# Layer 1's gates by extra product columns instead of elementwise GpSimd products, and its output bias by a one-row matmul

## The reference, cut to what matters

```python
local = _local_attention(heads(q), heads(k), heads(v))      # [B, H, S, 16]
...
lattn = jax.nn.softmax(lscores, axis=-1)
lat_out = jnp.einsum('bhsl,bhld->bhsd', lattn, rv)
remote = lat_out @ rout_w + rout_b
remote_h = remote.reshape(B, S, N_HEADS, HEAD_DIM).transpose(0, 2, 1, 3)
gate = jax.nn.sigmoid(local @ gl_w + remote_h @ gr_w)       # one number per token and head
mixed = gate * local + (1.0 - gate) * remote_h
mixed = mixed.transpose(0, 2, 1, 3).reshape(B, S, D)
return mixed @ out_w + out_b
```

## Time and profile before

| | |
|---|---|
| median of 3 runs | 1696.48 us (1692.83 to 1697.11) |
| the profiled execution | 1699.13 us |
| its span, first to last instruction | 1697.3 us |
| mean granted TensorE clock | 0.890 |
| busy: PE, DVE, ACT, POOL | 1348.5, 968.0, 602.7, 351.2 us |
| layer 1 | from about 924 us to the end |

### The profile page before, as it was taken

How to read it: one execution, slowest core, us unless ns; L and a number is a source line. 1 busy time by engine, 2 the same in 40 slices (tenths; PEclk the granted TensorE clock), 3 DMA queues, 4 the chain that set the end, 5 groups by cost and what they waited for, 6 DMA issues and landing times. The chain is left out here.

```text
span 1697.3 us, 24704 instructions
## 1 busy us (share of the span) xinstructions
PE 1348.5 (79%) x8765; PEld 849.9 (50%) x8765; DVE 968.0 (57%) x2253; ACT 602.7 (36%) x1137; POOL 351.2 (21%) x326
## 2 busy tenths in 40 slices
PE   4479898888888898309995699898989898988753
PEld 1234454454544454208995355646464646454532
DVE  4365555656555653505776166666766675666723
ACT  0034343434343445005552134343434343434331
POOL 2110111110111100161112221233333333312232
PEclk9789999999899989658998689899989998999866
DMA  3441315152522400482221432304040404030000
GB/s 121 115 114 46 94 45 135 45 135 73 121 81 53 100 21 2 157 264 75 75 60 41 131 97 64 95 32 107 33 106 31 108 33 107 24 94 14 2 13 13
DMA packets 70920, 130.40 MB, mean 77 GB/s; under 512 B 7936, under 2 KB 60816, under 8 KB 67344
## 3 DMA queue, kind: packets, MB, share of 16 engines
q1 hardware_dynamic: 67728, 120.42, 25.8%
q0 software_dynamic: 3072, 8.41, 1.8%
HBM read 84.19 MB, written 43.81 MB: 75 GB/s over the span
## 5 line engine op out<-in xcount | busy, mean ns | idle before, releaser
L473 DVE TENSOR_REDUCE first_maxima<-bank 128x1 f32<-128x512 f32 (+3 forms) x352 | 221.3, 638 | 243.4 <-PE bank L306 242.8
L427 ACT ACTIVATE arena<-pair 128x512 f32<-128x512 f32 x320 | 184.2, 598 | 338.2 <-PE pair L335 336.9
L1422 DVE TENSOR_REDUCE second_maxima<-bank 128x2 f32<-128x512 f32 (+1 forms) x224 | 152.7, 685 | 185.5 <-PE bank L1138 182.9
L1293 ACT ACTIVATE second_probs<-pair 128x512 f32<-128x512 f32 (+1 forms) x256 | 137.6, 541 | 307.9 <-PE pair L1162 299.1
L303 PE MATMUL bank<-first_k_stack,first_q_stack 96*128 96x256 bf16 (+3 forms) x512 | 131.8, 311 | 55.7 <-DVE first_maxima L473 36.0
L284 PE MATMUL bank<-first_xT,w_qkv 128*128 128x512 f32 x256 | 131.2, 640 | 17.0 <-DVE first_halves L458 12.9
L328 PE MATMUL pair<-first_q_stack,first_k_stack 99*128 99x512 bf16 (+3 forms) x512 | 125.5, 307 | 8.6 <-DMA first_q_stack<-first_m_turned 8.0
L540 POOL TENSOR_TENSOR first_halves<-first_halves 128x512 f32<-128x512 f32 x32 | 40.5, 1265 | 388.0 <-DVE first_halves L458 388.0
L1159 PE MATMUL pair<-second_q_stack,second_k_stack 99*128 99x256 bf16 (+1 forms) x512 | 99.5, 278 | 2.3 <-ACT second_probs L1293 2.3
L1136 PE MATMUL bank<-second_k_stack,second_q_stack 96*128 96x256 bf16 (+1 forms) x512 | 93.8, 278 | 8.5 <-DMA second_k_stack<-parked 6.6
L1162 PE MATMUL pair<-logits,constants_bf 128*128 128x512 bf16 (+1 forms) x256 | 98.2, 384 | 0.0
(11 more groups left out here) (313 smaller groups left out, 2509.1 us busy)
## 6 DMA issues: line engine op xcount, KB each, us to landing
parked<-first_parts SPq DMA_DIRECT2D x32, 384.0 KB, 2.8
first_q_stack<-parked SPq DMA_DIRECT2D x48, 256.0 KB, 5.0
first_k_stack<-parked SPq DMA_DIRECT2D x48, 256.0 KB, 8.0
parked<-second_parts SPq DMA_DIRECT2D x32, 384.0 KB, 2.5
second_q_stack<-parked SPq DMA_DIRECT2D x48, 256.0 KB, 5.0
second_k_stack<-parked SPq DMA_DIRECT2D x48, 256.0 KB, 7.9
sorted_x<-first_zero SPq DMA_DIRECT2D x3, 1670.5 KB, 11.7
expert_xs<-sorted_x SPq DMA_DIRECT2D x39, 128.5 KB, 2.3
```

Of the source, the lines that this page charges most:

```text
L427: act.activation(PT[:, s:s + len(heads), lo:lo + each], ex[n % 3][:, 0:len(heads) * each].rearrange("p (h q) -> p h q", h=len(heads)), ACT ...
L473: dve.tensor_reduce(nm[:, i, qt, heads[0]:heads[0] + len(heads)], mx[n % 2][:, 0:wide].rearrange("p (h k) -> p h k", h=len(heads)), AX.X, ...
L1293: act.activation(PT[:, s:s + len(heads), lo:lo + each], ex[n % 2][:, 0:len(heads) * each].rearrange("p (h q) -> p h q", h=len(heads)), ACT ...
L1422: dve.tensor_reduce(nm[:, i, qt, heads[0]:heads[0] + len(heads)], mx[n % 2][:, :].rearrange("p (h k) -> p h k", h=len(heads)), AX.X, ALU.m ...
```

## The change

The gate needs `local @ gl` and `remote @ gr`. Both are linear, so they are now made by TensorE as further columns:

- At the start VectorE forms, from the loaded weights, the value weights times gl (`wvg`, 16 columns for each of two chunks), `rout` times gr (`rout_g`), and both biases' products (`b_vg`, `b_rg`).
- A new piece "vg": eight matmuls of 16 columns (turned x by `wvg`) and two (latent values by `rout_g`), all into one bank; "vg_in" copies the latter to `RVG` and adds the former into column 17 of each head of V, where zeros stood. The second attention pass then carries the gate's local part along, and "norm" scales 18 columns for a head instead of 16.
- A new piece "rg": eight matmuls of 16 columns (latent probabilities by `RVG`), and "rg_in", which adds `b_rg`.
- "g_sum" is now one addition of 64 numbers on each partition. "u_r", "u_l" and "u_add" are gone from GpSimd; so is "xres". The output's bias is a matmul of one row by 512 columns at the end of each "out".
- "mix" writes into z, and "turn_a" reads z. "lt" and "lt_in" come 0.4 of a group earlier, "g_sum" to "mix" and "turn_a" to "new" somewhat earlier too.

```diff
@@ schedule1
-        at(g0 - 7.25, "xres", b)
+        at(g0 + 0.43, "vg", b)
+        at(g0 + 0.5, "vg_in", b)
+        at(g0 + 1.48, "rg", b)
+        at(g0 + 1.56, "rg_in", b)
-            at(g0 + 1.2 + 0.1 * i, "lt", b, i)
+            at(g0 + 0.8 + 0.1 * i, "lt", b, i)
-        at(t - 1.9, "u_r", b)
-        at(t + 0.8, "u_l", b)
-        at(t + 0.95, "u_add", b)
-            at(t + 1.45 + 0.1 * c, "turn_a", b, c)
+            at(t + 1.26 + 0.1 * c, "turn_a", b, c)
...
@@ TensorE
+                    elif kind == "vg":
...
+                        bank = claim("vg", b, 0)
+                        for t in range(NT):
+                            for c in range(KC):
+                                pe.matmul(bank[:, t * H:(t + 1) * H], xT[b % 2][:, c, t * P:(t + 1) * P], wvg[:, c, :],
+                                          start=(c == 0), stop=(c == KC - 1))
+                        for n in range(2):
+                            ins = pe.matmul(bank[:, (NT + n) * H:(NT + n + 1) * H],
+                                            BD[LD:2 * LD, 2 * n:2 * n + 2, :].rearrange("p h l -> p (h l)"),
+                                            rout_g[LD:2 * LD, :], start=True, stop=True)
+                        ins.then_inc(lp["vg_ps"], 1)
+                    elif kind == "rg":
...
+                        for t in range(NT):
+                            for n in range(2):
+                                ins = pe.matmul(bank[:, t * H:(t + 1) * H], LT[:, n, t * P:(t + 1) * P], RVG[:, n, :],
+                                                start=(n == 0), stop=(n == 1))
...
+                        ins = pe.matmul(bank[:, :], one_row[:, :],
+                                        w["b_out"][0:1, :].rearrange("p (r c) -> p r c", r=1).to_broadcast([1, 2, D]),
+                                        start=False, stop=True, skip_group_check=True)
@@ VectorE
+                        dve.tensor_copy(RVG[:, :, :], bank[:, NT * H:(NT + 2) * H].rearrange("p (n h) -> p n h", h=H)).then_inc(lp["rv_gate"], 1)
+                        dve.tensor_tensor(V[:, :, :, HD + 1], bank[:, 0:NT * H].rearrange("p (t h) -> p t h", h=H),
+                                          spread(b_vg[:, :], H, NT), ALU.add).then_inc(free, 1)
...
+                        dve.tensor_tensor(gs[:, :].rearrange("p (t h) -> p t h", h=H), A[:, :, :, HD + 1], Rg[:, :, :], ALU.add)\
+                            .then_inc(lp["g_sum"], 1)
-                        dve.wait_ge(lp["u"], b + 1)
-                        dve.tensor_reduce(gs[:, :], u1[:, :].rearrange("p (n c) -> p n c", c=HD), AX.X, ALU.add, negate=True)\
-                            .then_inc(lp["g_sum"], 1)
...
@@ GpSimd
-                    elif kind == "xres":
-                    elif kind == "u_r":
-                    elif kind == "u_l":
-                    elif kind == "u_add":
...
```

More of the change, by code:

```diff
@@ L901, in schedule1 @@
             at(t + 0.41 + 0.1 * i, "norm", b, i)
-        at(t + 0.8, "u_l", b)
-        at(t + 0.95, "u_add", b)
-        at(t + 1.0, "diff", b)
-        at(t + 1.1, "g_sum", b)
-        at(t + 1.15, "g_exp", b)
-        at(t + 1.22, "gate", b)
-        at(t + 1.3, "mix", b)
+        at(t + 0.75, "g_sum", b)
+        at(t + 0.8, "g_exp", b)
+        at(t + 0.84, "diff", b)
+        at(t + 0.95, "gate", b)
+        at(t + 1.05, "mix", b)
         for c in range(KC):
-            at(t + 1.45 + 0.1 * c, "turn_a", b, c)
-            at(t + 1.55 + 0.1 * c, "a_in", b, c)
-            at(t + 1.76 + 0.1 * c, "out", b, c)
-            at(t + 1.84 + 0.1 * c, "add", b, c)
+            at(t + 1.26 + 0.1 * c, "turn_a", b, c)
+            at(t + 1.35 + 0.1 * c, "a_in", b, c)
+            at(t + 1.66 + 0.1 * c, "out", b, c)
+            at(t + 1.74 + 0.1 * c, "add", b, c)
             at(t + 2.4 + 0.1 * c, "turn_z", b, c)
@@ L1363, in _ @@
                     dve.tensor_copy(mask, w[k]).then_inc(lp["masks"], 1)
+                flat = z[:, :, :].rearrange("p t c -> p (t c)")
+                for done, (out, src, gate, n) in enumerate(((wvg[:, :, :].rearrange("p k h -> p (k h)"), w["qkv"][:, :, 2 * D:3 * D], "gl", KC),
+                                          (rout_g[:, :], w["rout"].rearrange("p (k n) -> p k n", k=1), "gr", 1),
+                                          (b_vg[:, :], w["b_v"].rearrange("p (k n) -> p k n", k=1), "gl", 1),
+                                          (b_rg[:, :], w["b_rout"].rearrange("p (k n) -> p k n", k=1), "gr", 1))):
+                    if done:
+                        dve.wait_ge(lp["gates_set"], done)
+                    by_head = flat[:, 0:n * D].rearrange("p (k h c) -> p k h c", k=n, c=HD)
+                    for k in range(n):
+                        step(dve.tensor_tensor(by_head[:, k], src[:, k, :].rearrange("p (h c) -> p h c", c=HD), spread(w[gate], HD, H), ALU.mult))
+                    dve.tensor_reduce(out, flat[:, 0:n * D].rearrange("p (g c) -> p g c", c=HD), AX.X, ALU.add).then_inc(lp["gates_set"], 1)
+                dve.wait_ge(lp["gates_set"], 4)
                 dve.wait_ge(lp["bn"], 2)
```

103 lines of the change are left out of this document (59 added, 44 removed).

## The result

The changed kernel is slower. Its median was 1739.3 us against 1694.7 for the kernel before, a ratio of 1.028 (95% interval 1.021 to 1.036); run again beside the experiments it was 1743.1 against 1686.1, a ratio of 1.032 (1.028 to 1.036). The forecast was 1715, with 1706 to 1724 as its own range and 1733 as the slowest end. The direction was right, the size was not: a loss of 45 to 57 us where 18.5 were forecast.

The account below looks back on a forecast made before the run. TensorE's list of work was taken to set a batch's length. Added work 6.65 less saved waits 4.5 plus clock 0.35, over seven batches 17.5, last batch +1.5: +19 on 1696.5, about 1715 us, range 1706 to 1724.

Parts of the forecast that it names:

- what a batch gets more of: TensorE's additions per batch: narrow matmuls 4.2, bias matmul 1.7 and the wait behind "vg" 0.75, together 6.65 us.
- Narrow matmuls: The 16-column matmuls of "vg" and "rg" on TensorE: 36 more instructions, 4.2 us a batch.
- Bias matmul: Two one-row, 512-column matmuls a batch on TensorE, four instructions: 1.7 us more, no gain from having one row.
- "turn_a": Chain from last "norm" to "turn_a" falls from 13.5 to 7.3 us, TensorE's work meanwhile 7.2; wait saved 1.6 us.
- "turn_z": TensorE's 2.7 us wait before "turn_z" moves to "turn" and shrinks to 0.6 or 1.7; 1.3 us taken as saved.
- the better of the two cases: "split" runs freely beside GpSimd's root, saving 2.1 us at "turn_z"; if it must stand until the root ends, 1.0.
- The clock: Half-clock time shifts from falls at "turn_a" and "turn_z" to behind "vg": net +0.35 us a batch.
- the new wait: The second "turn_x" waits for the bank until VectorE finishes "vg_in": 0.75 us, between 0.3 and 1.5.
- much slower: the clock: Rival: "vg" and "rg" each lower the clock, falls at "turn" and "turn_a" stay; 1733 to 1741 us; chance 0.14 above 1724.
- The last batch: Last batch: 4.95 for products and "vg" wait, plus 2.6 for bias, less 6.0 from the shorter chain: +1.5 us.

Follow-up runs that it names:

- e5: The changed kernel run again without any edit: 1743.1 us, ratio 1.032 to the kernel before.
- e1: The changed kernel with "new_x" set back to t + 2.32, behind "mid" on GpSimd: 1706.9 us, ratio 1.012 to the kernel before.
- e4: The kernel before with only "new_x" moved to t + 2.24, ahead of "mid" on GpSimd: 1724.9 us, ratio 1.022.
- e12: e1 run again, profiled on the same chip as e11: 1710.7 us, ratio 1.011 to the kernel before.
- e3: e1 with "vg" and "rg" as one matmul each instead of 10 and 8, gates computed wrongly: 1661.3 us, ratio 0.984.
- e7: e6 without "xres" and with the changed kernel's one-row float32 bias matmul: 1691.9 us, ratio 1.002.
- e6: e2 with the remote half of the gate as product and sum on VectorE, without "rg": 1670.9 us, ratio 0.989.
- e11: The kernel before, unedited, profiled on the same chip as e12: 1694.5 us, ratio 1.002.
- e10: e9 with the local half of the gate on VectorE too, no "vg", "turn_a" somewhat later: 1636.5 us, ratio 0.968.
- e9: e6 with the two long VectorE instructions of the remote gate placed later: 1654.9 us, ratio 0.979.
- e2: e1 with the output bias back on GpSimd ("xres" restored, no bias matmul): 1679.3 us, ratio 0.994.

## Why the prediction missed

**The step that failed** is the sum of what a batch gets more of, 4.2 + 1.7 + 0.75 = 6.65 us: it puts at nothing, without a reason, what the moved instructions pass in GpSimd's queue. The runs showed a wait of 3.7 us for maxima in its place, in each of five batches, and the half clock behind it. The prediction told of GpSimd only that its products held up others and where the root stood; "new_x" has no term in it. The order of GpSimd after the change has "new_x" ahead of "mid"; asking of each moved instruction what it passes in its queue would have found 4.84 us in front of 0.61 us that VectorE waits for in order, with the score products behind. Its size, by the ratios of e5 and e1, is 1.032 against 1.012, about 34 us; e4 has it alone in the kernel before, 38.6 us. With it put right, e1 stands at 1.012 (1.007 to 1.017) and e12 at 1.011; the forecast's 1715 over 1696.5 is 1.011.

That agreement is partly luck, since its terms moved against one another:

*Narrow matmuls, 4.2 us a batch: right.* "vg" takes 2.3 us at full clock, as forecast, and e3 puts 32 of the 36 at 4.4 us in steady batches, some 3.2 without the clock. Here it is in the changed kernel, caught by a fall of the clock on its second half, with the wait of 0.46 us behind it for the bank:

```profile
1255.84 3.08 PE L1109 MATMUL pair<-second_wv_gate,second_xT 128*128 128x16 f32 x16 [0.24 <-DVE second_attended L1502]
1258.84 1.03 PE L1112 MATMUL pair<-second_rout_gate,second_block_diagonal 64*128 64x16 f32 x4
...
1260.34 1.12 PE L1055 MATMUL pair<-constants,second_x 128*128 128x128 f32 x4 [0.46 <-DVE second_values L1462]
```

*Bias matmul, 1.7 us: too small.* The two instructions take 1.05 us from start to next start, not 0.86; with what half clock adds (2.07 instead of 1.12 for one of them in the last batch of e12), e7 and e6 put it at 21 us in all, where the terms came to 14.5.

```profile
1287.02 1.12 PE L1227 MATMUL bank<-arena,second_one_row 1*128 1x512 f32 x2
1288.07 1.99 PE L1141 MATMUL bank<-second_rv_rout,second_latentT 128*128 128x256 f32 x8
```

*"turn_a": right.* From the last "norm" (end 1270.17) to the end of "mix" at 1277.40 there are 7.2 us, 7.3 forecast, and TensorE comes to "turn_a" 0.27 us later without waiting, so chain and work are equal indeed (left out between are "g_sum", "diff", "gate" and "split").

```profile
1269.71 0.46 DVE L1502 TENSOR_TENSOR second_attended<-bank,second_recips 128x288 f32<-128x288 f32 x1
...
1276.17 1.23 DVE L1526 TENSOR_TENSOR second_normed<-second_normed,second_remote 128x1024 f32<-128x1024 f32 x1
...
1277.67 0.60 PE L1217 MATMUL pair<-constants,second_normed 128*128 128x128 f32 x4
```

*"turn_z": the wait went as forecast, and the better of the two cases came.* "split" ran freely beside the root:

```profile
1298.08 1.67 POOL L1610 TENSOR_TENSOR second_rstd<-second_var_eps,minus_half 128x8 f32<-128x8 f32 x1 [18.71 <-DVE second_var_eps L1538]
...
1299.04 0.17 DVE L1492 TENSOR_TENSOR second_maxima<-second_maxima,second_m_parts 128x16 f32<-128x16 f32 x1
...
1299.78 0.16 DVE L1541 SCALAR_TENSOR_TENSOR second_minus_mean<-second_mean_var,second_rstd 128x2 f32<-128x2 f32 x1
```

The forecast gave the rule in the Trainium skill, "SBUF — State Buffer", section "SBUF: two separate sides", some weight. By it the row of "split" at 1299.04, with two SBUF operands, would have had to stand until 1299.75, the end of the root; it ran at 1299.04 for 0.17 us. The trace does not agree for this instruction, and the measurement decides. So the wait went from 2.7 to 0.5, a saving of 2.2, where the forecast had taken 1.3 as a value between its two cases, 2.1 and 1.0. In the trace small VectorE instructions of "split" run beside GpSimd's power seven times. In all 14 of them have two SBUF operands, and none took over 0.18 us.

*The clock: the mechanism right in part, the net sign wrong in e1.* The falls that begin in the four batches of e1 that the windows above show are 6.8, 3.4, 10.2 and 13.7 us at half clock, 8.5 a batch, worth 4.3. Behind "vg" begin 20.5 of these 34.1 us. Of the 6.8 in the first batch 3.4 begin only behind "pool", and the 10.2 begin at 1332.1, before "vg" at 1332.98, where TensorE had stood 2.0 us for the gather and 1.9 for "v_in". But the falls at "turn_a" and "turn_z" went wholly, 10.2 us a batch before, so e1 spends less time at half clock, not 0.35 us more. In the changed kernel itself the new wait brings falls of its own, and a steady batch has 18 us at half clock. The rival "much slower: the clock" gave 1733 to 1741, which is the number that came, but from "vg" and "rg" and falls at "turn" and "turn_a" that stay; its mark, a steady batch under 0.90, was met in two of four (0.87, 0.91, 0.89, 0.94). It came near the time by another mechanism.

*The last batch, +1.5: too small.* The chain shrank as worked out: from the last "norm" to "turn_a" 11.1 us before, 5.0 in e12. What went wrong is behind it. e12 from "turn_a" to the last "add", and e11 the same:

```profile
1668.06 1.12 PE L1217 MATMUL bank<-constants,second_normed 128*128 128x128 f32 x4 [6.04 <-DVE second_normed L1526]
...
1670.77 3.75 PE L1225 MATMUL bank<-arena,second_turned 128*128 128x256 f32 x8 [0.73 <-issue]
1674.45 2.07 PE L1227 MATMUL bank<-arena,second_one_row 1*128 1x512 f32 x2
1676.45 3.66 PE L1225 MATMUL bank<-arena,second_turned 128*128 128x256 f32 x8
...
1680.04 1.12 PE L1227 MATMUL bank<-arena,second_one_row 1*128 1x512 f32 x2
...
1681.20 0.69 DVE L1529 TENSOR_TENSOR second_x<-bank,second_x 128x512 f32<-128x512 f32 x1 [3.95 <-PE bank L1227]
```

```profile
1652.91 1.12 PE L1191 MATMUL pair<-constants,second_attended 128*128 128x128 f32 x4 [12.02 <-DVE second_attended L1463]
...
1655.62 3.60 PE L1199 MATMUL bank<-arena,second_turned 128*128 128x256 f32 x8 [0.73 <-issue]
1659.06 1.89 PE L1199 MATMUL pair<-arena,second_turned 128*128 128x256 f32 x8
...
1660.98 0.69 DVE L1467 TENSOR_TENSOR second_x<-pair,second_x 128x512 f32<-128x512 f32 x1 [1.03 <-PE pair L1199]
```

13.8 against 8.8 us from the first row to the last row's end. The bias is 3.2 of the 5.1 us, 2.6 forecast; the other 1.8 are the second "out", 3.66 where e11 had the clock back for it and took 1.89, and the last "up" took 3.78, all at half clock, against 1.12 + 1.03 at full clock. The bias matmul alone does not keep the clock down: with the same one before it the second "out" took 2.00 us in the changed kernel and 1.99 in e5 and e3, and 3.66 in e12, 3.78 in e1 and 3.77 in e7. What decides where the clock comes back is open. The batch's products ahead of the last "norm" cost 6.1, 4.95 forecast (the table of e11 and e12).

## What to carry to other kernels

When a change moves an instruction in a schedule of several in-order queues, list for each queue what it has moved past, and begin with the queue that has the longest pieces, here GpSimd's: 0.6 us of work behind 4.8 us cost 2% of the kernel through two other engines, and one number in the schedule decided it. Work moved from a slack engine onto the bound one needs a wait to fill on every occasion, the first and last included: e12 lost as much before its first gate as in six steady batches. Here both aims, a short chain and an idle GpSimd, were to be had from VectorE, which had room (e10, 3.2% faster than the kernel before), and where on it the work stands was worth another 16 us (e6 to e9).

## What was not expected of the hardware

- A matmul of 1 row and 512 columns in float32 is no cheaper than one of 128: its two instructions start 0.53 us apart on average, those of L1075 before 0.43. With three rows in bfloat16 it is 0.32 for one instruction.
- VectorE instructions of 16 elements, two of six with two SBUF operands, ran at 0.17 us beside GpSimd's power of 8 elements, in all seven batches that have such a pair and in e1 and e2 as well, while those beside GpSimd's products of 1024 stood still.
- The clock fell after 2.3 us of 16-column matmuls in a stretch where TensorE was busy 3.40 of 3.40 us, and stayed at 1.00 in e3, where one matmul of 96 columns stood in their place and TensorE was busy 8.92 of 10.20 us.
